# Eight units of a selective scan added by VectorE instead of twelve, and other places for the work between the scans

## The chip, the cores and the metric

One core of a Trainium2 chip runs the whole program. The metric is the device time of one execution in microseconds, from the start to the end of the program; the time of the kernel before is the median of three runs.

## The reference

Two layers in a row over x of shape (2, 4096, 512), in float32.

```python
def mixer(x, ...):                       # d_model 512, d_inner 1024, d_state 16, conv width 4, dt_rank 64
    xz = einsum('bld,ed->ble', x, in_proj_w);  xs, z = split(xz)
    xs = silu(causal_conv4(xs, conv_w) + conv_b)
    dt, B, C = split(einsum('bld,ed->ble', xs, x_proj_w), [64, 16, 16])
    dt = softplus(einsum('blr,dr->bld', dt, dt_proj_w) + dt_proj_b)
    A = -exp(A_log)                      # (1024, 16)
    h[t] = exp(dt[t] * A) * h[t-1] + dt[t] * B[t] * xs[t]      # state (1024, 16) for each batch
    y[t] = sum_n h[t][:, n] * C[t][n] + xs[t] * D
    return einsum('bld,ed->ble', y * silu(z), out_proj_w)
def ffn(x, ...):                         # weights quantised to -1, 0, 1
    return einsum('bsf,df->bsd', relu(einsum('bsd,fd->bsf', x, Wq1) + b1), Wq2) + b2
x = layernorm(x + mixer(x));  x = layernorm(x + ffn(x))
```

## The kernel before, in words

The program has two phases, one after the other. The change touches the first (`mixer_phase`) alone; `ffn_phase` is the same in both kernels.

**Tiling.** The 8192 tokens are cut into 16 chunks of 512, taken from the two batches in turn. In a chunk the 1024 channels are 8 blocks of 128 (the partitions), in 4 pairs q. A *unit* u (0 to 63) is one pair q = u // 16 and one state n = u % 16: two scans over 512 tokens, one for each block j of the pair. The body of a chunk is written once for every engine (`chunk`), as a loop over the 64 units; the first and the last chunk stand alone and the others are in a hardware loop of two chunks a turn. p, c and f are the chunk before, this one and the next: beside the scans of c run the output projection, residual and norm of p, and the input projection, convolution, x projection, dt projection and softplus of f.

**One unit through the engines.**
- ScalarE, `decay` (L488): exp(dt * A) into PSUM, one for each scan. There are two such banks; the decay of scan k waits until scan k - 2 is done.
- GpSimd, the product (L445): `dbu` = `dtx` * B for both blocks, in two buffers; it waits until both scans of unit u - 2 are done. In front of it GpSimd saves the last column of unit u - 2 (`carry`, L419).
- VectorE, `scan` (L696): twice a unit, into one of three slots of `h`. In front of the first it waits for the product, for the transposes and the carry of the unit that had the slot (three units back in most cases), and for the decay.
- TensorE, `transpose_h` (L871): four transposes for each half k of the unit, into PSUM `ht`, each half followed by one slot of other matmuls (`SLOTS`: two passes of 512 columns). The transposes wait for both scans of their unit, and for the reader of `ht` of the unit before.
- The reader multiplies by C. For most units it is ScalarE (`scale_by_c`, L502: four instructions of 128x256 into `ch`), and TensorE then adds the eight blocks to PSUM `y` (`sum_over_n`, L876). For the units in `BY_DVE` it is VectorE (`add_by_c`, L713 and L717: four instructions of 128x256 that add into `ya` in SBUF), and TensorE takes `ya` in only once for each pair q, at its last unit.

**The other work** stands at places written out by hand, one table for each operation (`TAKE_X`, `CONV_AT`, `ROUND_AT`, ...), each keyed by the unit u after whose instructions it is issued. On ScalarE: the first tap of the convolution (L510), SiLU of x (L516, four instructions and a table load), takes of PSUM banks (`take_xd` L521, `take_ct` L525, `take_dt` L532, `take_z` L552), the exponential of the softplus (L539 and L541), its logarithm (L546), SiLU of z (L557), and the norm's (L562, L566, L570). On VectorE: three taps a block and the copy that gives the bank back (L659, L667), `softplus_round` (L676, the rounding, and L678, the lift, behind one another), `softplus_sum` (L684), `skip` (L724), residual, statistics and shift (L731, L736, L742, L748). On GpSimd: the excess of the softplus (L384), `make_dtx` (L392), the gate with z (L379), the correction of the convolution (L400 to L413). SP issues all DMAs: B rows of a unit, weights of a block, tokens.

**Order on VectorE before.** In unit u: the statistics where they are due; scan 0; taps 2 and 3 of a block; the add of unit u - 1, if VectorE has it (for units 10, 38, 54 and 60 it stands in front of scan 0 of the next, `ADD_FIRST`); scan 1; then tap 1, skips, rounding with lift, sum, residual and shift. On ScalarE in unit u: decay of u + 1 and scaling of u - 1 for k = 0, the same for k = 1, and then all the rest that is due at u.

## Time and profile before

| | us |
|---|---|
| median of three runs | 5273.15 (5272.78 to 5276.83) |
| profiled execution, its own time | 5271.46 |
| its span, first to last instruction | 5269.7 |
| first scan of the first chunk | 83.8 |
| first scan of the sixth chunk, and of the seventh | 1347.3, 1601.5 |
| last scan ends | 4143.4 |

The rows are from one profiled execution. In a view of groups, a row gives line, engine, operation, output and inputs, the shape, the count, the busy time, the mean ns of one, and the idle time of the engine just before them with what ended it. In the timeline, a row gives start and length in us, and in brackets how long the engine had been idle and what released it. Busy times of windows are unions; the matmul records overlap one another at their ends, so what one costs TensorE is read from the distance of starts.

### The profile page before, as it was taken

To read this page: it belongs to the slowest core of one execution; us is meant where nothing else is said; L and a number is where in the kernel's file an instruction comes from. 1 tells how busy PE (TensorE), PEld (TensorE's weight loads), DVE (VectorE), ACT (ScalarE), POOL (GpSimd) and SP (SyncE) were. 2 spreads that over 40 slices of the span, in tenths; PEclk is the share of its full clock that TensorE was granted. 3 is DMA by queue.
4 is the path that set the end of the run, shared out by engine and by line. 5 is a ranking of instruction groups with operands and counts; after the bars stand their busy time and mean duration, and the time that the engine had idled before them with its cause. 6 is when DMAs were issued, how large, how long until landed. Compare 5 with 4: busy or idle time off the path is not lost. (4 is left out here: it accounts for less than half of the span.)

```text
span 5269.7 us, 85222 instructions
## 1 busy us (share of the span) xinstructions
PE 4539.6 (86%) x23362; PEld 3148.9 (60%) x23362; DVE 4053.4 (77%) x4775; ACT 3573.7 (68%) x6726; POOL 3171.4 (60%) x2474
## 2 busy tenths in 40 slices
PE   5989897988888888879797979797987579999998
PEld 3656555555555555656564656565656357777777
DVE  5888888888888888888898989898988554444444
ACT  5888787878787878787887787878787412222222
...
GB/s 96 97 91 91 100 92 99 90 99 92 104 86 107 95 97 93 96 98 91 97 96 104 84 101 87 103 89 101 88 91 89 130 2 32 41 39 32 32 32 32
DMA packets 233272, 436.64 MB, mean 83 GB/s; under 512 B 23872, under 2 KB 24000, under 8 KB 232320
## 3 DMA queue, kind: packets, MB, share of 16 engines
...
## 5 line engine op out<-in xcount | busy, mean ns | idle before, releaser
L696 DVE TENSOR_TENSOR_SCAN h<-decay,carry,dbu 128x512 f32<-128x512 f32 x2048 | 2528.8, 1269 | 313.6 <-ACT decay L488 144.4
L445 POOL TENSOR_TENSOR dbu<-dtx,bb 128x1024 f32<-128x1024 f32 x1024 | 2462.3, 2405 | 5.5 <-issue 2.2
L488 ACT ACTIVATE decay<-dt,aneg 128x512 f32<-128x512 f32 x2048 | 1431.3, 701 | 692.6 <-DVE h L696 688.0
L871 PE MATMUL ht<-ident,h 128*128 128x128 f32 x8192 | 1338.9, 291 | 609.7 <-DVE h L696 462.2
L871 PEld LDWEIGHTS ht<-ident,h 128*128 128x128 f32 x8192 | 1012.0, 149 | 1329.4 <-issue 812.6
L502 ACT ACTIVATE ch<-ht,ct 128x256 f32<-128x256 f32 x3328 | 1404.0, 482 | 93.3 <-PE ht L871 91.5
L821 PE MATMUL gemm<-xt,win 128*128 128x512 f32 x2048 | 1067.6, 606 | 10.8 <-DMA win<-w_in 7.1
L876 PEld LDWEIGHTS y<-ident,ch 128*128 128x128 f32 x6656 | 790.3, 143 | 407.3 <-issue 364.1
L876 PE MATMUL y<-ident,ch 128*128 128x128 f32 x6656 | 893.1, 278 | 4.2 <-ACT ch L502 1.9
L419 POOL TENSOR_TENSOR carry<-h,ones_pair 128x2 f32<-128x2 f32 x1022 | 272.0, 266 | 856.7 <-DVE h L696 846.9
L1119 ACT ACTIVATE hr<-hidden_ps,b1c 128x512 f32<-128x512 f32 x256 | 176.4, 689 | 715.8 <-PE hidden_ps L1252 715.8
L855 PE MATMUL gemm<-wout,x 128*128 128x512 f32 x1024 | 529.3, 604 | 0.0
L1201 DVE CAST hhi<-hr 128x512 fp32r<-128x512 f32 x256 | 109.3, 427 | 496.1 <-ACT hr L1119 496.0
L1263 PE MATMUL out_ps<-w2q,hhi 128*128 128x512 f32 x1024 | 409.1, 400 | 2.8 <-DVE hlo L1203 2.6
L1252 PE MATMUL hidden_ps<-xhi,w1q 128*128 128x512 f32 x1024 | 407.4, 398 | 1.4 <-DVE xlo L1164 1.4
L1252 PE MATMUL hidden_ps<-xlo,w1q 128*128 128x512 f32 x1024 | 407.3, 398 | 0.0
L1263 PE MATMUL out_ps<-w2q,hlo 128*128 128x512 f32 x1024 | 404.0, 395 | 0.0
L821 PEld LDWEIGHTS gemm<-xt,win 128*128 128x128 f32 x2048 | 319.3, 196 | 28.0 <-issue 20.9
L717 DVE SCALAR_TENSOR_TENSOR ya<-ht,ct,ya 128x256 f32<-128x256 f32 x512 | 221.4, 477 | 120.9 <-PE ht L871 119.8
L659 DVE SCALAR_TENSOR_TENSOR x<-gemm,cw,x 128x511 f32<-128x511 f32 (+2 forms) x384 | 281.3, 733 | 20.8 <-ACT x L510 16.0
L1263 PEld LDWEIGHTS out_ps<-w2q,hhi 128*128 128x128 f32 x1024 | 193.4, 189 | 54.0 <-issue 8.6
L1252 PEld LDWEIGHTS hidden_ps<-xhi,w1q 128*128 128x128 f32 x1024 | 193.0, 189 | 50.3 <-DVE xlo L1164 1.8
...
## 6 DMA issues: line engine op xcount, KB each, us to landing
bb<-b_rows SPq DMA_DIRECT2D x1024, 256.0 KB, 3.3
win<-w_in SPq DMA_DIRECT2D x256, 256.0 KB, 3.7
...
```

The source lines that it names most:

```text
L419: nc.gpsimd.tensor_tensor(carry[:, c.par, n, pair(q)], h[:, H_SLOT[u], :, TC - 1], ones[:, :], ALU.mult)\
L445: nc.gpsimd.tensor_tensor(dbu[:, u % 2, :, :], dtx[:, pair(q), :], bb[:, u % BB_RING:u % BB_RING + 1, :].to_broadcast([P, 2, TC]), ALU.mul ...
L488: nc.scalar.activation(DA[j][:, :], dt[:, c.par, i, :], ACT.Exp, scale=aneg[:, i, n:n + 1])\
L502: ins = nc.scalar.activation(ch[:, b % 2, tb, :], HT[k][:, tb % 2, :], ACT.Copy, scale=ct[:, c.par, tb, n:n + 1])
L659: nc.vector.scalar_tensor_tensor(x[:, f.par, i, back:], G[BANK["x", i]][:, 0:TC - back], cw[:, i, KC - 1 - back:KC - back], x[:, f.par, i, ...
L696: nc.vector.tensor_tensor_scan(h[:, H_SLOT[u], j, :], DA[j][:, :], dbu[:, u % 2, j, :], carry[:, c.par, n, i:i + 1], ALU.mult, ALU.add).th ...
L821: ins = nc.tensor.matmul(G[BANK[kind, i]][:, :], win[:, slot, k, :], xt[:, chunk.par, k, :], start=(k == 0), stop=(k == KM - 1))
L855: ins = nc.tensor.matmul(G[BANK["o", tb]][:, :], x[:, p.par, i, tb * P:(tb + 1) * P], wout[:, i, :], start=(i == 0), stop=(i == NB - 1))
L871: ins = nc.tensor.transpose(HT[k][:, tb % 2, j * P:(j + 1) * P], h[:, H_SLOT[u], j, tb * P:(tb + 1) * P], ident[:, :])
L876: return nc.tensor.matmul(Y[j][:, tb * P:(tb + 1) * P], src, ident[:, :], start=begins and tb == 0, stop=False, is_transpose=True, skip_gr ...
L1252: ins = nc.tensor.matmul(HP[j % 2][:, :], w1q[:, k, j * P:(j + 1) * P], part[:, k, :], start=(k == 0 and part is xhi), stop=(k == KM - 1 a ...
L1263: ins = nc.tensor.matmul(OP[tb][:, :], part[:, j % 2, tb * P:(tb + 1) * P], w2q[:, j, :], start=(j == 0 and part is hhi), stop=(j == NJ - ...
```

## The change

`BY_DVE` goes from twelve units to eight, and the tables give finer places. ScalarE's are keyed by 2u + k (after half k of unit u), VectorE's by 3u + s (s = 0 in front of scan 0, 1 between the scans, 2 behind scan 1), GpSimd's by u as before. Every add has a place of its own in `ADD_AT` (`ADD_FIRST` is gone), every tap, statistic and skip too, and the lift is split from the rounding, with its own semaphore. The tables for TensorE and SP are the same.

```diff
-BY_DVE = (9, 10, 20, 37, 38, 39, 53, 54, 55, 59, 60, 61)
-ADD_FIRST = (11, 39, 55, 61)
+BY_DVE = (9, 21, 39, 51, 52, 53, 55, 59)
...
-TAKE_X = {20 + 2 * i: i for i in range(NB)}
-CONV_AT = {21 + 2 * i: i for i in range(NB)}
-SILU_X_AT = 37
-TAKE_Z = {3: 0, 36: 1, 38: 2, 44: 3, 52: 4, 54: 5, 56: 6, 58: 7}
-TAKE_XD_AT, TAKE_CT_AT = 43, 46
-TAKE_DT = {47 + i: (2 * i, 2 * i + 1) for i in range(NB // 2)}
-EXP_AT = {48: 0, 50: 1, 3: 2, 5: 3}
-ROUND_AT = {50: 0, 52: 1, 5: 2, 7: 3}
-LN_AT = {53: (0, 1), 9: (2, 3)}
-EXCESS_AT = {56: 0, 57: 1, 12: 2, 13: 3}
-DT_SUM_AT = {56: 0, 57: 1, 12: 2, 13: 3}
-DTX_AT = {60: 0, 61: 1, 4: 2, 6: 3, 18: 4, 20: 5, 22: 6, 24: 7}
-SILU_Z_AT = 59
-GATE_AT = {61: (0, 1), 62: (2, 3), 63: (4, 5), 3: (6, 7)}
-SKIP_AT = {NS * (q + 1) + 2: q for q in range(NP - 1)}
-RESIDUAL_AT = {7 + 4 * tb: tb for tb in range(TB)}
-STATS_AT, NORM_LN_AT, SHIFT_AT = 39, 53, 54
-NORM_AT = {56: (0,), 57: (1, 2), 58: (3,)}
-CORR_AT, FIX_AT = 2, 38
+TAKE_X = {41: 0, 45: 1, 47: 2, 53: 3, 58: 4, 60: 5, 65: 6, 68: 7}
+SILU_X_AT = 80
+TAKE_Z = {8: 0, 72: 1, 76: 2, 91: 3, 109: 4, 113: 5, 115: 6, 116: 7}
+TAKE_XD_AT, TAKE_CT_AT = 85, 92
+TAKE_DT = {94: (0, 1), 95: (2,), 96: (3,), 97: (4,), 100: (5, 6), 101: (7,)}
+EXP_AT = {2: 2, 9: 3, 97: 0, 102: 1}
+LN_AT = {21: (2, 3), 105: (0, 1)}
+SILU_Z_AT = 118
+NORM_LN_AT = 105
+NORM_AT = {111: (0,), 113: (1,), 117: (2,), 121: (3,)}
+ADD_AT = {32: 9, 68: 21, 124: 39, 159: 51, 161: 52, 168: 53, 170: 55, 183: 59}
+CONV_AT = {65: ((0, 1),), 66: ((0, 2),), 67: ((0, 3),), 69: ((1, 1),), 71: ((1, 2),), 73: ((1, 3),), 76: ((2, 1),),
+           79: ((2, 2),), 82: ((2, 3),), 85: ((3, 1), (3, 2)), 87: ((3, 3),), 93: ((4, 1),), 94: ((4, 2), (4, 3)), 96:
+           ((5, 1),), 97: ((5, 2),), 98: ((5, 3),), 101: ((6, 1),), 103: ((6, 2),), 105: ((6, 3),), 106: ((7, 1), (7,
+           2)), 110: ((7, 3),)}
+ROUND_AT = {23: (2,), 29: (3,), 151: (0,), 160: (1,)}
+LIFT_AT = {14: (2,), 30: (3,), 156: (0,), 158: (1,)}
+DT_SUM_AT = {36: 2, 48: 3, 177: 0, 180: 1}
+SKIP_AT = {7: ((3, 0), (3, 1)), 54: ((0, 0),), 56: ((0, 1),), 105: ((1, 0), (1, 1)), 152: ((2, 0),), 154: ((2, 1),)}
+RESIDUAL_AT = {26: 0, 37: 1, 48: 2, 64: 3}
+STATS_AT = {85: (0,), 96: (1,), 114: (2,), 115: (3,)}
+NORM_SUMS_AT, SHIFT_AT = 151, 167
+EXCESS_AT = {12: 2, 15: 3, 56: 0, 57: 1}
+DTX_AT = {1: (2,), 11: (3,), 16: (4,), 18: (5,), 20: (6,), 25: (7,), 60: (0,), 61: (1,)}
+GATE_AT = {3: (6,), 6: (7,), 60: (0, 1), 61: (2,), 62: (3, 4), 63: (5,)}
+CORR_AT, FIX_AT = 10, 39
...
-                wait(act, rounded_ready, f, 2 * NP, 2 * q + 2)
+                wait(act, rounded_ready, f, NP, q + 1)
+                wait(act, lifted, f, NP, q + 1)
...
                 if j == 0:
-                    wait(dve, dbu_ready, c, UNITS, u + 1)
                     back, user = h_user_before(u)
                     wait(dve, ht_full, c.near(back), HALVES, 2 * user + 2)
                     wait(dve, carried, c.near(back), UNITS, user + 1)
+                    wait(dve, decay_ready, c, SCANS, 2 * u + 1)
+                    wait(dve, dbu_ready, c, UNITS, u + 1)
+                else:
+                    wait(dve, decay_ready, c, SCANS, 2 * u + 2)
...
                 for u in range(UNITS):
+                    between(3 * u)
                     scan(c, u, 0)
+                    between(3 * u + 1)
                     scan(c, u, 1)
+                    between(3 * u + 2)
```

`between(at)` issues what is due at `at` in the order add, taps, skips, roundings, lifts, sum, residual, statistics, their aggregation, shift.

## Rows read from the trace of the kernel before

**Rows 1.** The page: busy us, share of the span and instructions of each engine.

```profile
PE 4539.6 (86%) x23362; PEld 3148.9 (60%) x23362; DVE 4053.4 (77%) x4775; ACT 3573.7 (68%) x6726; POOL 3171.4 (60%) x2474
```

**Rows 2.** Windows: busy us of PE, PEld, DVE, ACT, POOL, then PEclk, DMA share, GB/s.

```profile
1347.30:1393.60 46.30, 41.49 (x234) 28.24 (x233) 39.36 (x41) 39.06 (x73) 41.05 (x35) 0.97 0.32 104
1393.60:1431.60 38.00, 36.86 (x203) 24.67 (x202) 33.22 (x32) 27.05 (x58) 32.98 (x25) 0.96 0.24 77
1431.60:1481.30 49.70, 47.85 (x271) 32.23 (x270) 49.42 (x59) 42.26 (x90) 36.42 (x30) 1.00 0.31 104
1481.30:1510.90 29.60, 22.41 (x107) 13.71 (x106) 23.99 (x37) 20.00 (x33) 15.27 (x14) 0.88 0.23 77
1510.90:1578.10 67.20, 59.42 (x319) 37.67 (x318) 56.24 (x55) 59.16 (x116) 50.59 (x37) 0.97 0.26 80
1578.10:1601.50 23.40, 10.49 (x63) 8.19 (x61) 17.34 (x22) 18.65 (x30) 22.30 (x19) 0.72 0.54 169
```

**Rows 3.** Groups by line of VectorE and ScalarE, in one chunk, 1347.3 to 1601.5.

```profile
L696 DVE TENSOR_TENSOR_SCAN h<-decay,carry,dbu 128x512 f32<-128x512 f32 x128 | 158.0, 1269 | 20.0 <-ACT decay L488 8.7 <-POOL carry L419 6.5 <-POOL dbu L445 3.7
...
L717 DVE SCALAR_TENSOR_TENSOR ya<-ht,ct,ya 128x256 f32<-128x256 f32 x32 | 13.9, 478 | 8.0 <-PE ht L871 8.0
...
L713 DVE TENSOR_SCALAR ya<-ht,ct 128x256 f32<-128x256 f32 x16 | 7.0, 479 | 5.6 <-PE ht L871 5.6
...
L676 DVE TENSOR_SCALAR rounded<-soft 128x1024 f32<-128x1024 f32 x4 | 4.8, 1210 | 0.0
...
L502 ACT ACTIVATE ch<-ht,ct 128x256 f32<-128x256 f32 x207 | 87.2, 481 | 4.0 <-PE ht L871 3.9
```

**Rows 4.** Timeline of TensorE, unit 14 and the start of 15.

```profile
1405.38 0.60 PE L871 MATMUL ht<-ident,h 128*128 128x128 f32 x4
...
1407.99 1.04 PE L876 MATMUL y<-ident,ch 128*128 128x128 f32 x8
...
1408.87 0.60 PE L871 MATMUL ht<-ident,h 128*128 128x128 f32 x4
```

**Rows 5.** Groups by line of VectorE in units 36 to 42, 1481.3 to 1510.9.

```profile
L717 DVE SCALAR_TENSOR_TENSOR ya<-ht,ct,ya 128x256 f32<-128x256 f32 x8 | 3.5, 480 | 3.2 <-PE ht L871 3.2
...
L736 DVE BATCH_NORM_STATS2 stats<-xres 128x6 f32<-128x512 f32 x4 | 2.5, 679 | 0.0
...
L713 DVE TENSOR_SCALAR ya<-ht,ct 128x256 f32<-128x256 f32 x4 | 1.8, 480 | 0.9 <-PE ht L871 0.9
```

**Rows 6.** Timeline of GpSimd at the end of the chunk, two products.

```profile
1589.05 2.35 POOL L445 TENSOR_TENSOR dbu<-dtx,bb 128x1024 f32<-128x1024 f32 x1
...
1593.94 2.36 POOL L445 TENSOR_TENSOR dbu<-dtx,bb 128x1024 f32<-128x1024 f32 x1
```

**Rows 7.** Timeline at SiLU of x, and TensorE after an idle time.

```profile
1489.98 1.28 ACT L516 ACT_TABLE_LOAD   x1
...
1491.27 3.90 ACT L516 ACTIVATE x<-x 128x1024 f32<-128x1024 f32 x4
...
1496.49 1.30 ACT L488 ACTIVATE decay<-dt,aneg 128x512 f32<-128x512 f32 x2
...
1502.07 1.11 PE L871 MATMUL ht<-ident,h 128*128 128x128 f32 x4 [5.75 <-DVE h L696]
```

**Rows 8.** Timeline at units 48 and 49, what ends just before a scan.

```profile
1524.86 2.36 POOL L445 TENSOR_TENSOR dbu<-dtx,bb 128x1024 f32<-128x1024 f32 x1
...
1527.54 2.46 DVE L696 TENSOR_TENSOR_SCAN h<-decay,carry,dbu 128x512 f32<-128x512 f32 x2 [0.34 <-POOL carry L419]
...
1530.39 0.79 ACT L488 ACTIVATE decay<-dt,aneg 128x512 f32<-128x512 f32 x1
...
1531.21 2.62 DVE L696 TENSOR_TENSOR_SCAN h<-decay,carry,dbu 128x512 f32<-128x512 f32 x2 [1.21 <-ACT decay L488]
```

**Rows 9.** One line each: rounding and dt sum, ns min/median/max.

```profile
L676 DVE TENSOR_SCALAR rounded<-soft x64: 665/895/2250, 67.6 to 3944.0; 128x1024 f32<-128x1024 f32 x64
L684 DVE SCALAR_TENSOR_TENSOR dt<-soft,dt x64: 1190/1199/3343, 74.4 to 3970.4; 128x1024 f32<-128x1024 f32 x64
```

More of the change, by code:

```diff
@@ L228, in mixer_phase @@
         rounded_ready = sem("rounded_ready")
+        lifted = sem("lifted")
         ln_ready = sem("ln_ready")
@@ L634, in _ @@
+                        if at == NORM_LN_AT and not is_first:
+                            norm_ln(p)
+                            norm_exp(p)
+                        if not is_first:
+                            for tb in NORM_AT.get(at, ()):
+                                norm_apply(p, tb)
+                        if at == SILU_Z_AT:
+                            silu_z(c)
             walk(act, chunk)
@@ L757, in _ @@
                 softplus_round(first, q)
+                softplus_lift(first, q)
             for q in (0, 1):
```

151 lines of the change are left out of this document (74 added, 77 removed).

## The prediction

> **What bounds the kernel now.** I read the page first. It shows four engines at 60 to 86 per cent of the whole span [rows 1], an average over two programs: the page's chain of waits runs through the second phase, which the change leaves alone. The first phase has sixteen chunks, and its clock is the start of VectorE's scans. So I took one chunk without a disturbance, from 1347.3 to 1601.5 us, 254.2 us long, and asked the view of windows for six stretches of it [rows 2]: units 0 to 12, 12 to 22, 22 to 36, 36 to 42, 42 to 59 and 59 to 64. The reader is to see that the limit moves. In the second and third TensorE is busy 36.9 of 38.0 and 47.9 of 49.7 us, and VectorE 49.4 of 49.7. In the fourth nobody is (VectorE 24.0 of 29.6). In the fifth ScalarE leads (59.2 of 67.2), VectorE just behind (56.2). In the last it is GpSimd (22.3 of 23.4). Over the chunk VectorE works 219.6 us and is idle for some 34.6. The groups by line [rows 3] say before what: 20.0 us before scans (8.7 for a decay, 6.5 and 3.7 by GpSimd), and 8.0 + 5.6 = 13.6 us before the adds of the twelve units, always for TensorE's transposes.
>
> **TensorE's floor.** A full unit is four transposes, a slot, four transposes, a slot and eight summing transposes; in the timeline the next unit starts at 1408.87 after 1405.38, which is 3.49 us, of which the eight summing ones are 0.88 (1407.99 to 1408.87) [rows 4]. A unit added by VectorE has no such sum and costs 2.61. Units 0 to 35 fill every slot: 36 x 3.49 = 125.6, plus three sums of `ya` and two dropped units' difference: after, 125.6 + 3 x 0.88 - 2 x 0.88 = 126.5 us (before 125.6, with three dropped). They take 134.0 us now (the first three windows).
>
> **Part 1, eight units instead of twelve.** VectorE loses 16 instructions. 48 of them are busy 13.9 + 7.0 = 20.9 us [rows 3], 0.435 each: -7.0 us of its work a chunk. ScalarE gets 16 scalings at 87.2 / 207 = 0.42 [rows 3]: +6.7 us. TensorE gets 4 sums, +3.5 us. None of the three is a change of time by itself; each counts in the stretch where that engine is last.
>
> **Part 2, adds later.** An add now stands between the two scans one unit on, or in front of them. Its transposes need both scans of its unit and then stand on either side of a slot, so VectorE comes too early for each half: in units 36 to 42 it idles 3.2 + 0.9 us before the pieces of three adds [rows 5]. The new places are one scan to two units later, when the transposes are there. I take 10 of the 13.6 us as gone and 3.6 as staying (unit 55's, unit 39's).
>
> **Part 3, by stretch.** *Units 0 to 36.* The wait for units 9, 10 and 20 goes, and the two exponentials, two roundings and gates that stand close together in units 3 to 7 are spread. But TensorE leaves only 134.0 - 126.5 = 7.5 us to win. Against that stand new waits: the sum of `dt` is now in front of unit 12's scan, and needs an excess that GpSimd makes after that unit's product; it is late by about one half product, 1.4 us (a product is 2.35) [rows 6]. Taps of the convolution are spread over more units, so the banks of blocks 2 and 6 are given back later, 1 to 2 us for TensorE. I take -4.0; bounds 0 and -7.5.
> *Units 36 to 42.* Out go the adds of 37 and 38 (8 x 0.435 = 3.5), the statistics of two blocks and the aggregation (1.5, moved into earlier units where TensorE covers them) and the 4.1 us of waits before adds; four statistics are busy 2.5 us [rows 5]. In comes a bare SiLU of x. It takes ScalarE from 1489.98, a table load of 1.28 and 3.90 of work, and then another load, to the next decay at 1496.49 [rows 7]: 6.5, with a decay on each side 7.8 us from the scan that releases it to the one it releases. Now the adds of 37 and 38 and the statistics cover it. After, only scan, scan (1.2 from one to the next: three in a row are over in 3.6) and the add of 39 (4 x 0.435) lie beside it: 1.2 + 1.2 + 1.7 = 4.1. Uncovered 3.7. Sum -3.5 - 1.5 - 4.1 + 3.7 = -5.4; bounds -1.3 (none of the waits goes) and -9.1 (SiLU hidden).
> *Units 42 to 59.* One more add here, so VectorE +1.7, ScalarE 1.7 less. The take of xd stands one unit earlier, at the end of unit 42, and TensorE ends that product only then; ScalarE holds the next decays behind it: +2.2. The exponentials now stand between two decays of one unit instead of after both, so VectorE has one scan less as cover. Against that the waits before three adds go. I take +1.5; bounds -6 and +7.
> *Units 59 to 64.* GpSimd has five products, two `dtx` and six gates before and after. From one product to the next with two gates between is 1593.94 - 1589.05 = 4.89 us [rows 6] and it is busy 22.3 of the 23.4 us [rows 2]; moving gates within five units frees nothing. SiLU of z stands half a unit earlier with less cover, but it hides behind GpSimd: +0.5; bounds -1 and +2.
>
> **Part 4, the product waited for last.** The scan's waits are separate; the last one is cheap. A decay ends at 1530.39 + 0.79 = 1531.18 and the scan starts at 1531.21, 0.03 us later; a product ends at 1524.86 + 2.36 = 1527.22 and its scan starts at 1527.54, 0.32 us later [rows 8]. That second row names the carry as releaser, but the carry is three units old and passed; it is the product. So 0.29 is to be had where the 3.7 + 6.5 us of waits for GpSimd stand, at some twelve places, 3.5 us; where GpSimd or TensorE is last, it isn't passed on. I take -0.5 (bounds 0 and -3.5).
>
> **Part 5, GpSimd's own instructions** change in place, not in number: no DMA is moved, and SP's queue keeps its order; only its waits for banks follow TensorE.
>
> **Sum.** -4.0 - 5.4 + 1.5 + 0.5 - 0.5 = -7.9 us a chunk. Each new place has its own small release, which I price at +0.5: -7.4. The first chunk has no norm before it and the last no next chunk, so fifteen of sixteen: 15 x -7.4 = -111. The profiled execution took 5271.5 us (its span 5269.7 and 1.8 around it); it is 1.7 below the median 5273.15. 5273 - 111 = 5162, and I say **5160 us**. The bounds add up to -27 and +8 a chunk; five errors seldom fall together, so the forecast's own range goes a quarter of the way to each, -12 and -3.5: 5273 - 15 x 12 = 5093 to 5273 - 15 x 3.5 = 5220.
>
> **A rule weighed: who holds the port.** A rounding takes from 665 to 2250 ns, a `dt` sum from 1190 to 3343, for one shape [rows 9]. In this chunk the four roundings average 1210 [rows 3], so 4 x 0.545 = 2.2 us are waits inside them, and if one sum of the four is of the long sort, 2.15 more: 4.3. "SBUF — State Buffer" of the Trainium skill, section "SBUF: two separate sides", says that a VectorE operation in a two-port mode or with two SBUF inputs and a GpSimd operation exclude one another, and that whichever starts first keeps the pair to its end. By that rule the trace agrees (the excess is of a product's length), and the change isn't neutral: the lift stood right behind its rounding, and now takes its turn alone. I left this out of the sum, since the places behind a second scan come before the next product starts, and the two roundings between scans come in the midst of one.
>
> **Rivals.**
> *A: smaller gain, 5240.* TensorE takes back nearly all of units 0 to 36 (-1), SiLU and the take of xd cost what they can: -1 - 3 + 2.3 - 0.5 = -2.2; 15 x -2.2 = -33. For: TensorE has +3.5 us more and is at 96 per cent in two windows. Against: 36 to 42 doesn't hang on it. Chance 0.19.
> *B: larger gain, 5035.* The first stretch reaches TensorE's floor, SiLU is half hidden, and the fifth gains a little: -7.5 - 7 - 1 - 0.5 = -16; 15 x -16 = -240. For: after an idle of 5.75 us, TensorE's four transposes take 1.11 instead of 0.60 [rows 7, 4], and the granted clock of the windows with such gaps is 0.88 and 0.72 [rows 2], between its levels of 1.2 and 2.4 GHz; shorter gaps give that back. Against: four engines within 10 per cent of each other. Chance 0.13.
> *C: slower, ScalarE late.* The mechanism is that exponentials, SiLU and xd stand between two decays of one unit; VectorE has one scan (1.2) to cover 2.1 to 6.5 us. If cover is what the old places had, units 36 to 59 lose 2.2 (xd) + 3 x 1.2 + 3.7, less the 4 that the adds give back: +5.5, and the first stretch gives nothing: 5273 + 15 x 5.5 = 5355. It decides where the waits before scans for a decay pass 20 us a chunk (8.7 now). For: ScalarE is at 59.2 of 67.2 already. Against: its load there falls by 1.7. Chance 0.08.
> *D: slower, the port.* If each of the twelve roundings, lifts and sums waits out half a product (1.2), that is 14.4 for 4.3: +10, which eats the -7.4: 5273 + 15 x 2.7 = 5314. The page of the Trainium skill named above, "SBUF — State Buffer", is where this comes from. It decides when the mean excess of the twelve is over (4.3 + 7.4) / 12 = 0.98 us. Against: eight of twelve stand where a scan has just ended. Chance 0.05.
> *E: nothing,* the parts cancel within 0.2 per cent, 10.5 us, which is about what a measurement of this kernel can tell from no change: 5273, 0.04.
>
> **How the numbers follow.** Forecast 0.51, A 0.19, B 0.13, C 0.08, D 0.05, E 0.04. Faster by over 0.2 per cent: 0.51 + 0.19 + 0.13 = 0.83; same 0.04; slower 0.13. The range leaves 0.10 above (C and most of D) and 0.10 below (the far part of B): 5070 to 5265; the forecast's own is 5093 to 5220.
>
> **What would show it.** Right: the idle before `ya` falls under 4 us a chunk; stretch 36 to 42 takes 22 to 25 us; 59 to 64 stays at 23 to 24; releases by the product come at 0.03 to 0.1; TensorE is idle under 4 us in units 12 to 36. Wrong: stretch 42 to 59 over 72 us (C); the mean rounding over 1.7 us or lift over 1.6 (D); or units 0 to 36 not under 132 us, which would mean that TensorE's floor was hit from another side.

## The result, and the profile after

The kernel after takes 5245.74 us, median of five runs (5234.61 to 5249.39), beside 5273.15 (5270.68 to 5291.18) for the kernel before on the same chip: a ratio of 0.9937, 95% interval 0.9918 to 0.9957. That is 27 us less. The forecast was 5160, 113 less; the time lies inside the range given (5070 to 5265), and next to rival A's 5240. The direction was right, and the size was four times too large: that the time lies inside the range says little, since the range also held rival A.

The profiled execution of after took 5243.3 us. The page's line of busy times answers to [rows 1]:

```profile
PE 4566.3 (87%) x23874; PEld 3192.9 (61%) x23874; DVE 3851.1 (73%) x4519; ACT 3673.4 (70%) x6982; POOL 3179.2 (61%) x2474
```

VectorE has 202 us less to do, ScalarE 100 more, TensorE 27 more. Now one chunk in the six stretches of [rows 2], 1355.7 to 1608.5 (252.8 us). The columns are busy us of PE, PEld, DVE, ACT and POOL, then the clock, the DMA share and GB/s:

```profile
1355.70:1400.70 45.00, 40.88 (x225) 27.95 (x226) 37.38 (x37) 40.13 (x77) 38.45 (x34) 0.96 0.31 98
1400.70:1435.80 35.10, 34.49 (x196) 23.31 (x195) 29.70 (x29) 28.57 (x63) 32.86 (x25) 1.00 0.24 73
1435.80:1489.10 53.30, 50.24 (x287) 33.98 (x286) 51.76 (x66) 41.14 (x85) 35.58 (x28) 1.00 0.38 110
1489.10:1512.90 23.80, 20.84 (x117) 13.44 (x115) 18.22 (x21) 22.32 (x40) 15.34 (x13) 1.00 0.30 93
1512.90:1583.40 70.50, 59.74 (x307) 37.08 (x308) 54.83 (x64) 58.70 (x114) 50.30 (x37) 0.95 0.24 73
1583.40:1608.50 25.10, 13.36 (x83) 11.69 (x81) 14.85 (x17) 21.83 (x38) 23.23 (x19) 0.80 0.44 145
```

Three stretches are shorter than in [rows 2] and three longer: 46.3, 38.0, 49.7, 29.6, 67.2, 23.4 became 45.0, 35.1, 53.3, 23.8, 70.5, 25.1. One chunk of each can mislead, since chunks of one execution differ (250.4 to 256.8 us in after, 253.7 to 262.8 in before). So the next table has the means of fourteen chunks (the second to the fifteenth), from start to start of the scans that bound the stretches; it also holds the experiments, in the order in which they come below. The last column is the whole run.

```
us per chunk    0-6   6-12  12-22  22-36  36-42  42-52  52-59  59-64   chunk   ratio [95%]
before        24.61  23.81  38.06  49.78  29.42  35.90  31.17  23.71  256.46   1
after         21.25  23.21  35.41  53.25  23.84  39.70  31.75  26.21  254.62   0.9937 [0.9918, 0.9957]
a_wait        21.91  23.03  35.67  53.22  23.83  39.38  31.46  26.37  254.86   0.9960 [0.9946, 0.9973]
b_wait        24.00  23.68  38.07  49.36  29.20  36.29  31.22  23.65  255.46   0.9968 [0.9955, 0.9981]
a_xd          21.60  22.94  35.20  53.27  23.84  38.16  32.68  26.17  253.86   0.9903 [0.9887, 0.9918]
a_zg          22.15  23.39  35.52  53.27  23.83  39.62  31.64  24.67  254.08   0.9905 [0.9889, 0.9921]
a_conv        21.42  23.27  34.44  52.11  24.54  39.47  31.49  26.38  253.11   0.9883 [0.9865, 0.9902]
b_by8         24.02  22.48  39.94  50.03  25.97  38.83  30.56  23.28  255.12   0.9940 [0.9923, 0.9956]
h2            22.21  23.60  34.75  52.11  24.54  38.08  32.09  25.52  252.89   0.9867 [0.9849, 0.9884]
h3            22.59  22.94  34.40  52.11  24.54  41.52  30.14  25.54  253.78   0.9921 [0.9905, 0.9937]
b_by8w        23.98  22.47  38.81  49.68  25.95  39.17  30.18  23.06  253.31   0.9914 [0.9901, 0.9927]
a_stats       21.32  22.94  35.19  52.31  24.16  39.45  31.93  26.31  253.61   0.9931 [0.9919, 0.9944]
h6            20.68  23.41  34.75  50.94  25.92  39.19  30.18  23.07  248.14   0.9751 [0.9738, 0.9763]
h7            21.35  23.21  34.51  50.95  26.50  38.20  32.66  23.38  250.76   0.9821 [0.9808, 0.9835]
```

Before to after: units 0 to 22 -6.6, 22 to 36 +3.5, 36 to 42 -5.6, 42 to 59 +4.4, 59 to 64 +2.5: -1.8 a chunk. Fourteen such chunks give -26; the first is 5.2 longer, the last 9.2 shorter and the first scan 2.1 later, so the last scan ends at 4115.8 where it was 4143.4: -27.6. Each row of the table is one profiled execution, and how far its cells can be trusted shows in units 0 to 22: the ten kernels with the new places there take 78.8 to 81.1 us for them, the four with the old ones 85.3 to 86.5. So the 6.6 us are real, and a difference under some 1 us in that stretch is not.

What VectorE waits for has changed hands. Two rows of the page for the scan, first before, then after (busy us, mean ns, idle us just before, and the releaser with the most of it):

```profile
L696 DVE TENSOR_TENSOR_SCAN h<-decay,carry,dbu 128x512 f32<-128x512 f32 x2048 | 2528.8, 1269 | 313.6 <-ACT decay L488 144.4
```

```profile
L714 DVE TENSOR_TENSOR_SCAN h<-decay,carry,dbu 128x512 f32<-128x512 f32 x2048 | 2538.3, 1270 | 593.9 <-ACT decay L497 416.6
```

And in the chunk of the windows, the groups that answer to [rows 3]:

```profile
L714 DVE TENSOR_TENSOR_SCAN h<-decay,carry,dbu 128x512 f32<-128x512 f32 x129 | 160.0, 1270 | 40.7 <-ACT decay L497 26.3 <-POOL dbu L454 8.9 <-issue 4.8
...
L511 ACT ACTIVATE ch<-ht,ct 128x256 f32<-128x256 f32 x224 | 93.9, 477 | 7.4 <-PE ht L898 7.3
...
L731 DVE TENSOR_SCALAR ya<-ht,ct 128x256 f32<-128x256 f32 x16 | 6.8, 473 | 2.3 <-PE ht L898 2.2
L735 DVE SCALAR_TENSOR_TENSOR ya<-ht,ct,ya 128x256 f32<-128x256 f32 x16 | 6.7, 473 | 2.2 <-PE ht L898 2.2
```

(The 4.8 us of "issue" are one gap, just in front of the chunk's first scan; over the fourteen chunks they come to 0.3 a chunk.) The reader is to see three things. The adds wait 4.5 us where they waited 13.6: that part came as planned. The adds' work fell from 20.9 to 13.5 us, as planned too. But the scans wait 26.3 us for a decay of ScalarE where it was 8.7. In the fourteen-chunk means VectorE works 207.3 us a chunk where it worked 220.5, and its idle time rose from 35.9 to 47.3 (for a decay 9.4 to 27.0, before adds 13.6 to 5.3): most of what was taken from VectorE became waiting for ScalarE.

**Where ScalarE comes late.** The take of xd, in the timeline of after; it stands behind the second decay of unit 43 and in front of the first of unit 44:

```profile
1516.31 0.85 ACT L511 ACTIVATE ch<-ht,ct 128x256 f32<-128x256 f32 x2
...
1518.49 1.02 PE L858 MATMUL gemm<-x,wxp 128*96 128x512 f32 x2
...
1519.55 0.60 ACT L530 ACTIVATE rounded<-gemm 96x512 f32<-96x512 f32 x1 [2.39 <-PE gemm L858]
1520.05 0.67 ACT L497 ACTIVATE decay<-dt,aneg 128x512 f32<-128x512 f32 x1
...
1520.85 1.28 DVE L714 TENSOR_TENSOR_SCAN h<-decay,carry,dbu 128x512 f32<-128x512 f32 x1 [2.75 <-ACT decay L497]
```

ScalarE itself stands idle for 2.39 us, because TensorE ends the x projection only at 1519.51; the decay behind the take comes late by that, and the first scan of unit 44 waits 2.75 (3.5 in the mean of fourteen chunks). The second place is SiLU of z, between the decays of unit 60:

```profile
1585.85 0.70 ACT L497 ACTIVATE decay<-dt,aneg 128x512 f32<-128x512 f32 x1
...
1586.85 1.28 DVE L714 TENSOR_TENSOR_SCAN h<-decay,carry,dbu 128x512 f32<-128x512 f32 x1
1587.32 1.28 ACT L567 ACT_TABLE_LOAD   x1
...
1588.61 3.90 ACT L567 ACTIVATE z<-z 128x1024 f32<-128x1024 f32 x4
1589.83 2.50 POOL L388 TENSOR_TENSOR x<-x,z 128x512 f32<-128x512 f32 x2 [1.77 <-ACT z L567]
...
1592.43 2.35 POOL L454 TENSOR_TENSOR dbu<-dtx,bb 128x1024 f32<-128x1024 f32 x1
1592.53 1.28 ACT L497 ACT_TABLE_LOAD   x1
1593.82 0.69 ACT L497 ACTIVATE decay<-dt,aneg 128x512 f32<-128x512 f32 x1
...
1594.55 1.28 DVE L714 TENSOR_TENSOR_SCAN h<-decay,carry,dbu 128x512 f32<-128x512 f32 x1 [6.42 <-ACT decay L497]
...
1595.32 1.12 PE L898 MATMUL ht<-ident,h 128*128 128x128 f32 x4 [7.31 <-ACT ch L511]
```

Decay, a scaling, load, SiLU, load, decay are one row on ScalarE, and VectorE has only the scan of 1.28 us beside them: it stands 6.42 us, TensorE 7.31. GpSimd's product for the next unit is late as well, since it is queued behind gates that wait for z (1.77 idle, and the product starts only at 1592.43).

**Table loads.** Each of the 164 loads of this trace takes 1.28 us, and here each starts 0.02 us behind the instruction before it and the next one 0.01 us behind the load, so SiLU with both loads is 1.28 + 3.90 + 1.28 = 6.5 us. "ScalarE: Activation LUTs" of the Trainium skill, section "What ACT_TABLE_LOAD costs", gives the same 1283 ns for the load but adds a drain to some 2.66 us for each switch; by that the piece would be 9.2. This trace doesn't show the drain, and the measurement decides.

### The profile page after: what moved, and what is told of

It is laid out like the page before. It is cut to its first block and busy times, and to the rows that moved or that the text cites. A ratio compares the mean times of both kernels' runs of the same rounds, so it can differ in the third digit from the quotient of the medians.

```text
span 5241.6 us, 86246 instructions
## 1 busy us (share of the span) xinstructions
PE 4566.3 (87%) x23874; PEld 3192.9 (61%) x23874; DVE 3851.1 (73%) x4519; ACT 3673.4 (70%) x6982; POOL 3179.2 (61%) x2474
## 5 line engine op out<-in xcount | busy, mean ns | idle before, releaser
L898 PE MATMUL ht<-ident,h 128*128 128x128 f32 x8192 | 1301.6, 284 | 469.0 <-ACT ch L511 330.9
L898 PEld LDWEIGHTS ht<-ident,h 128*128 128x128 f32 x8192 | 992.4, 146 | 1131.1 <-ACT ch L511 581.5
L511 ACT ACTIVATE ch<-ht,ct 128x256 f32<-128x256 f32 x3584 | 1505.9, 479 | 122.3 <-PE ht L898 120.9
L903 PEld LDWEIGHTS y<-ident,ch 128*128 128x128 f32 x7168 | 860.9, 145 | 443.3 <-issue 403.1
L848 PE MATMUL gemm<-xt,win 128*128 128x512 f32 x2048 | 1083.9, 614 | 20.9 <-DVE hist L679 13.7
L903 PE MATMUL y<-ident,ch 128*128 128x128 f32 x7168 | 976.1, 280 | 12.4 <-DVE x L741 12.0
L428 POOL TENSOR_TENSOR carry<-h,ones_pair 128x2 f32<-128x2 f32 x1022 | 258.0, 252 | 814.0 <-DVE h L714 802.0
L1279 PEld LDWEIGHTS hidden_ps<-xhi,w1q 128*128 128x128 f32 x1024 | 193.1, 189 | 50.3 <-DVE xlo L1191 1.8
L1279 PEld LDWEIGHTS hidden_ps<-xlo,w1q 128*128 128x128 f32 x1024 | 193.1, 189 | 47.0
```

Of the source, the lines that this page charges most:

```text
L428: nc.gpsimd.tensor_tensor(carry[:, c.par, n, pair(q)], h[:, H_SLOT[u], :, TC - 1], ones[:, :], ALU.mult)\
L511: ins = nc.scalar.activation(ch[:, b % 2, tb, :], HT[k][:, tb % 2, :], ACT.Copy, scale=ct[:, c.par, tb, n:n + 1])
L848: ins = nc.tensor.matmul(G[BANK[kind, i]][:, :], win[:, slot, k, :], xt[:, chunk.par, k, :], start=(k == 0), stop=(k == KM - 1))
L898: ins = nc.tensor.transpose(HT[k][:, tb % 2, j * P:(j + 1) * P], h[:, H_SLOT[u], j, tb * P:(tb + 1) * P], ident[:, :])
L903: return nc.tensor.matmul(Y[j][:, tb * P:(tb + 1) * P], src, ident[:, :], start=begins and tb == 0, stop=False, is_transpose=True, skip_gr ...
L1279: ins = nc.tensor.matmul(HP[j % 2][:, :], w1q[:, k, j * P:(j + 1) * P], part[:, k, :], start=(k == 0 and part is xhi), stop=(k == KM - 1 a ...
```

## The experiments

Theory T1: the adds and statistics of VectorE had covered ScalarE's long pieces, and what the change takes off VectorE's path there comes back as waiting for a decay. T2: ScalarE's load (the sum of its work) is a floor in units 42 to 64, whatever the places. The rival to both: the order of the scan's waits, or TensorE, took the gain back. T1 and T2 mean these two down to b_by8w, whose expectation gives them another wording.

**a_wait and b_wait: the order of the scan's waits.** a_wait is after with the old order, b_wait before with the new one. In b_wait:

```diff
                 if j == 0:
-                    wait(dve, dbu_ready, c, UNITS, u + 1)
                     wait(dve, ht_full, c.near(back), HALVES, 2 * user + 2)
                     wait(dve, carried, c.near(back), UNITS, user + 1)
+                    wait(dve, decay_ready, c, SCANS, 2 * u + 1)
+                    wait(dve, dbu_ready, c, UNITS, u + 1)
+                else:
+                    wait(dve, decay_ready, c, SCANS, 2 * u + 2)
-                wait(dve, decay_ready, c, SCANS, 2 * u + j + 1)
```

> The changed kernel with the old order of waits in front of the first scan (product first, decay last). Theory 'the order pays': each of some 9 releases by the product in a chunk costs 0.29 us more, the period of a chunk grows by 1 to 2.5 us, and the time from 5246 to 5260-5285, over the kernel before. Rival 'another engine is last there': under 0.5 us a chunk, 5240-5253; the releases are later and TensorE or GpSimd hides it.

> The kernel before with the new order of waits alone (product last). Theory 'the order pays': the 3.8 + 4.6 us of waits for GpSimd a chunk fall by up to 3.5, the time by 15 to 50, to 5225-5258. Rival 'another engine is last': 5265-5275, the waits only change their name.

Measured: a_wait 0.9960 [0.9946, 0.9973], b_wait 0.9968 [0.9955, 0.9981]. The order alone makes the kernel before 0.3% faster, 16 us; taken out of after it costs about 0.2%, with intervals that overlap. Neither expectation was met cleanly: b_wait's 5263 lies between its two bands, and a_wait's 5258 is 2 us short of the theory's, while its chunk grows by only 0.2 us, which is the rival's mark. What the order does to a single release is clear. In after a product that comes last releases its scan 0.04 us after its end (1602.23 + 2.37 = 1604.60), where [rows 8] had 0.32:

```profile
1602.23 2.37 POOL L454 TENSOR_TENSOR dbu<-dtx,bb 128x1024 f32<-128x1024 f32 x1
...
1604.64 2.46 DVE L714 TENSOR_TENSOR_SCAN h<-decay,carry,dbu 128x512 f32<-128x512 f32 x2 [2.46 <-POOL dbu L454]
```

Over the whole traces, the scans that had to wait for their product start 0.32 us behind its end in before and a_wait (median of 188 and 129) and 0.035 us in after and b_wait (141 and 174). So the order didn't take the gain back. In b_wait it is worth 1.0 us a chunk, twice the 0.5 that the prediction took; in after its worth is not settled.

**a_xd: the take of xd one unit later.**

```diff
-TAKE_XD_AT, TAKE_CT_AT = 85, 92
+TAKE_XD_AT, TAKE_CT_AT = 87, 92
```

> The changed kernel with one edit: the take of xd one unit later, after unit 43 (TAKE_XD_AT 85 to 87), as in the kernel before. Theory 'work between decays': the 3.3 us wait in unit 43 falls under 1, units 42 to 52 go from 39.7 to 36.5-37.5 us, the time from 5246 to 5195-5220. Rival 'ScalarE's load': it has 16 scalings more whatever their place, so units 42 to 52 stay at 39-40 and the time within 10 us.

Measured: 0.9903 [0.9887, 0.9918], 5232 us, 13 under after and outside both bands. The wait in front of unit 44, 3.5 us, is gone, and units 42 to 52 are 1.5 shorter (38.2 where 36.5 to 37.5 was expected); 0.9 of it comes back in 52 to 59. The wait was a matter of place, but of 3.5 us only 0.6 stay as a gain in 42 to 59. That the rest comes back is not shown to be ScalarE's load, as T2 has it: in units 42 to 59 of this kernel ScalarE is busy 58.9 of 70.8 us, and 6.0 of its idle time are waits for TensorE's transposes in front of a scaling.

**a_zg: SiLU of z and the gates at their old places.**

```diff
-SILU_Z_AT = 118
+SILU_Z_AT = 119
-GATE_AT = {3: (6,), 6: (7,), 60: (0, 1), 61: (2,), 62: (3, 4), 63: (5,)}
+GATE_AT = {3: (6,), 6: (7,), 61: (0, 1), 62: (2, 3), 63: (4, 5)}
```

> The changed kernel with SiLU of z at the end of unit 59 (118 to 119) and the gates where they were (two after each of units 61, 62, 63), as in the kernel before. Theory 'work between decays': the 6.4 us wait in unit 60 falls to 2-3.5, GpSimd's product of unit 61 no longer stands behind two gates, units 59 to 64 go from 26.2 to 23-24 us, the time from 5246 to 5200-5220. Rival 'GpSimd's sum is the floor': the stretch has the same five products, two dtx and six gates, and stays at 25-26; time within 10 us.

Measured: 0.9905 [0.9889, 0.9921], 5231 us, 11 above the expected band. Units 59 to 64 give 1.5 of the 2.5 us that they had lost (24.7 for the 23 to 24 expected), but in this trace units 0 to 22 are 1.2 longer, so the chunk is 0.5 shorter. The first scan of unit 61, which now stands behind SiLU of z, still waits 5.1 us. The add of unit 60, which had lain there, is not in the list of eight; h6 and h7 below show what it makes of that wait.

**a_conv: the convolution as before.** The first taps stand four half units apart again, and the other taps of a block close together.

```diff
-TAKE_X = {41: 0, 45: 1, 47: 2, 53: 3, 58: 4, 60: 5, 65: 6, 68: 7}
-CONV_AT = {65: ((0, 1),), 66: ((0, 2),), 67: ((0, 3),), 69: ((1, 1),), 71: ((1, 2),), ...
+TAKE_X = {41 + 4 * i: i for i in range(NB)}
+CONV_AT = {65: ((0, 1),), 67: ((0, 2), (0, 3)), 71: ((1, 1),), 73: ((1, 2), (1, 3)), ...
```

> The changed kernel with the convolution where it was: first taps on ScalarE after every second unit from 20, VectorE's first tap behind the second scan, the other two and the copy between the next unit's scans. Theory 'banks': the spread taps give a bank back up to two units later, and TensorE, the last engine here, waits for the copy; undone, units 22 to 36 go from 53.3 to 49.7-50.3 us, the time from 5246 to 5190-5210. Rival 'TensorE's floor': its extra sums make 14 x 3.49 + 0.9 = 49.7 us anyway, and what is lost was lost before; the stretch stays above 52, time within 10 us.

Measured: 0.9883 [0.9865, 0.9902], 5220 us, 26 under after, the largest step by the places of one operation. It misses the 5190 to 5210 of the theory, and units 22 to 36 take 52.1 us where the theory had 49.7 to 50.3 and the rival over 52. 1.1 us came from units 22 to 36 and 1.0 from 12 to 22 (which is within what that stretch varies by); 36 to 42 paid 0.7. So the spread taps cost something, and are a third of what units 22 to 36 had lost, not all of it.

**b_by8: the kernel before with eight adds, nothing moved.**

```diff
-BY_DVE = (9, 10, 20, 37, 38, 39, 53, 54, 55, 59, 60, 61)
-ADD_FIRST = (11, 39, 55, 61)
+BY_DVE = (9, 20, 37, 38, 53, 54, 59, 60)
+ADD_FIRST = (39, 55, 61)
```

> The kernel before with four units fewer on VectorE (10, 39, 55 and 61 go to ScalarE) and nothing moved. Theory 'the adds were cover': VectorE works 7.0 us less a chunk, but at 39, 55 and 61 ScalarE is in a long block (SiLU, logarithm), so waits for a decay rise from 9.0 by about what the adds lose: the chunk moves by less than 2 us, 5250-5290, and only units 6 to 12 shrink. Rival 'work is work': VectorE is the most loaded engine, and 4 to 7 us a chunk go, 5170-5215.

Measured: 0.9940 [0.9923, 0.9956], 5248 us, the gain of the whole change, by two lines; 2 us under the theory's band and far above that of "work is work". Its scans wait 13.4 us a chunk for a decay and not 27.0. The expectation that only units 6 to 12 shrink failed in a way that matters: units 36 to 42 fall by 3.5 us, and 42 to 52 grow by 2.9, though in 42 to 52 nothing was moved and no add was dropped. TensorE is about half a unit further behind when unit 42 starts (40.4 units transposed where it was 41.0), and in 42 to 52 it is busy 38.2 of 38.8 us (before 35.3 of 35.9). ScalarE is busy 37.0 there and waits 1.5 for its transposes, where it waited for none. What the adds leave in 36 to 42 is for the most part taken back there, and TensorE is the engine that is full. So the other places of the change, taken together, bring nothing over this, although units 0 to 22 are 6.6 us shorter with them.

**h2 and h3: the mends together, with more adds.** h2 is after with the convolution, xd, SiLU of z and the gates as before, and units 60 and 61 added by VectorE as well (ten units). h3 is h2 with units 48 and 49 too; with unit 48 on VectorE no product starts PSUM `y` afresh for the last pair any more: h3 leaves out that start and the wait in front of it, and `y` of that pair is no longer the sum alone, so its time is of use only as a hint.

```diff
-BY_DVE = (9, 21, 39, 51, 52, 53, 55, 59)
-ADD_AT = {32: 9, 68: 21, 124: 39, 159: 51, 161: 52, 168: 53, 170: 55, 183: 59}
+BY_DVE = (9, 21, 39, 48, 49, 51, 52, 53, 55, 59, 60, 61)
+ADD_AT = {32: 9, 68: 21, 124: 39, 149: 48, 152: 49, 159: 51, 161: 52, 168: 53, 170: 55, 181: 59, 183: 60, 187: 61}
```

> The changed kernel with the three parts put right: convolution as before, take of xd after unit 43, SiLU of z and gates as before, and units 59, 60 and 61 added by VectorE (ten units; adds between the scans of 60, in front of 61, between the scans of 62). If the stretches add up: 79.9 (0 to 22, as changed) + 49.8 (22 to 36) + 23.8 + 70.8 (36 to 59, as with xd moved) + 23.7 = 248.0 us a chunk, 5246 - 15 x 6.6 = 5147, 5130-5170. Rival 'waits move': ScalarE is the floor from 42 on and takes back what 22 to 36 gives, 5190-5220.

> As the one with three parts put right, and VectorE adds units 48 and 49 too (behind the scans of 49 and 50), where it waits 2.9 and 3.6 us for ScalarE. Theory 'ScalarE is last in 42 to 52': its 8 scalings less, 3.4 us, shorten units 42 to 52 by 1.5 to 3.4 us: 5100-5140. Rival 'TensorE's lag': ScalarE waits there for dt blocks, nothing or a loss: 5140-5180.

Measured: h2 0.9867 [0.9849, 0.9884], 5209 us and not the 5147 expected; h3 0.9921 [0.9905, 0.9937]. Both miss. In h2 two stretches carry most of the miss: 22 to 36 takes 52.1 us, as in a_conv, for the 49.8 expected, and 59 to 64 takes 25.5 for 23.7. There the adds of 60 and 61 didn't help: a_zg, with the same places of SiLU of z and the gates and without these adds, takes 24.7. Two adds at 48 and 49 made 42 to 52 longer by 3.4 (and 52 to 59 shorter by 2.0): VectorE there waits 3.3 us until TensorE has finished `y` of the pair before. To put cover in wherever ScalarE is late does not work by itself.

**b_by8w: the two parts that had worked, together.** b_by8 with the wait order of b_wait.

> The kernel before with the eight adds (units 9, 20, 37, 38, 53, 54, 59, 60) at the old kind of place and the product waited for last; nothing else is moved. T1 (ScalarE's long pieces stand uncovered; the places of the change bring nothing net): the two parts that were measured alone add up, 0.9940 x 0.9968 = 0.991, that is about 5230 us, under the whole change's 5246. T2 (the new places carry the gain and only the order of the waits hides it): about 5248, as without the order.

Measured: 0.9914 [0.9901, 0.9927], 5229 us. 0.9940 x 0.9968 = 0.9908: the two add up, as its T1 has it, and this kernel is at 0.9914 where after is at 0.9937 (the intervals just overlap), though it moves nothing.

**a_stats: the statistics back in one place**, in front of unit 41's first scan.

```diff
-STATS_AT = {85: (0,), 96: (1,), 114: (2,), 115: (3,)}
-NORM_SUMS_AT, SHIFT_AT = 151, 167
+STATS_AT = {123: (0, 1, 2, 3)}
+NORM_SUMS_AT, SHIFT_AT = 123, 167
```

> The kernel after with the four blocks' statistics and their aggregation back in one place, behind unit 40's add (slot 123), where VectorE waits for the SiLU of x. Theory (VectorE is full in units 22 to 36, so work moved there is paid in full, while in 36 to 42 it had hidden SiLU): stretch 22 to 36 falls by 1.4 us (two blocks' statistics of 0.63 each and a little), 36 to 42 by 0.5 to 1.3 or at least doesn't grow, since the aggregation leaves 42 to 59: 2.0 to 2.6 us a chunk, 5205 to 5215 us. Rival (TensorE covers them there, as the prediction had it): 22 to 36 stays at 53.2 and 36 to 42 grows by up to 2.5: 5246 to 5285.

Measured: 0.9931 [0.9919, 0.9944]; the expected 5205 to 5215 was missed (5237). Units 22 to 36 fall by 0.9, two thirds of the 1.4 us of work that left them; 36 to 42 grow by 0.3 with four statistics and the sums in them where there were two, so most of what was put there lies beside SiLU of x. The theory's fall in 22 to 36 is there at two thirds, but it had 36 to 42 not growing, and the whole is within the interval of after. What is new in units 22 to 36 shows in VectorE's groups there, of after and then of before:

```profile
L714 DVE TENSOR_TENSOR_SCAN h<-decay,carry,dbu 128x512 f32<-128x512 f32 x29 | 36.1, 1267 | 1.4 <-ACT decay L497 1.4
...
L731 DVE TENSOR_SCALAR ya<-ht,ct 128x256 f32<-128x256 f32 x4 | 1.6, 468 | 0.0
...
L753 DVE BATCH_NORM_STATS2 stats<-xres 128x6 f32<-128x512 f32 x2 | 1.4, 684 | 0.0
```

```profile
L696 DVE TENSOR_TENSOR_SCAN h<-decay,carry,dbu 128x512 f32<-128x512 f32 x28 | 34.4, 1268 | 0.0
```

VectorE had no idle time before a scan here in the kernel before, and 1.4 us in the one after. The add of unit 21 (1.6) and two statistics (1.4) are new in the stretch, which grew by 3.5. By the runs most of that work is paid, though not all: 0.9 for the statistics (a_stats), 1.3 for the add (h6, below), and 1.1 for the taps (a_conv).

**h6: units 0 to 21 from after, the rest from before.** Units 0 to 21 as in after, everything from unit 22 on as in before (convolution too), the eight units 9, 21, 37, 38, 53, 54, 59, 60, and the new wait order. Against after:

```diff
-BY_DVE = (9, 21, 39, 51, 52, 53, 55, 59)
+BY_DVE = (9, 21, 37, 38, 53, 54, 59, 60)
-ADD_AT = {32: 9, 68: 21, 124: 39, 159: 51, 161: 52, 168: 53, 170: 55, 183: 59}
+ADD_AT = {32: 9, 68: 21, 115: 37, 117: 38, 163: 53, 165: 54, 181: 59, 183: 60}
-SILU_X_AT = 80
+SILU_X_AT = 75
-STATS_AT = {85: (0,), 96: (1,), 114: (2,), 115: (3,)}
-NORM_SUMS_AT, SHIFT_AT = 151, 167
+STATS_AT = {117: (0, 1, 2, 3)}
+NORM_SUMS_AT, SHIFT_AT = 117, 164
-SILU_Z_AT = 118
+SILU_Z_AT = 119
...
```

> The places of the kernel after for units 0 to 21, those of the kernel before from unit 22 on (convolution too), eight units added by VectorE (9, 21, 37, 38, 53, 54, 59, 60), the product waited for last. If the stretches are separate sums (theory: each place pays or costs where it stands), 0 to 22 takes the 80 us of after, 22 to 36 about 50.5, 36 to 64 what the eight units at old places gave (119): 249.5 us a chunk, about 5165 us. Rival (the gain of the first 22 units is time lent by the end of the chunk before, ScalarE and GpSimd being late there): 0 to 22 goes back toward 83 or 42 to 64 grows, in all 252 to 253 us, 5200 to 5220.

Measured: 0.9751 [0.9738, 0.9763], 5147 us, 99 under after and 126 under before, and 18 better than expected. Its stretches are those of after for 0 to 22 (78.8; after 79.9) and those of b_by8w behind (36 to 64: 118.4; 118.4). So the 6.6 us are not lent by the end of the chunk before. Units 22 to 36 take 1.3 more than in b_by8w, about the add of unit 21 that now lies in them. SiLU of z in this kernel:

```profile
1551.17 1.28 DVE L711 TENSOR_TENSOR_SCAN h<-decay,carry,dbu 128x512 f32<-128x512 f32 x1 [1.14 <-ACT decay L494]
...
1552.65 0.88 DVE L732 SCALAR_TENSOR_TENSOR ya<-ht,ct,ya 128x256 f32<-128x256 f32 x2 [0.20 <-PE ht L895]
1553.16 1.28 ACT L564 ACT_TABLE_LOAD   x1
...
1553.98 0.88 DVE L732 SCALAR_TENSOR_TENSOR ya<-ht,ct,ya 128x256 f32<-128x256 f32 x2 [0.46 <-PE ht L895]
1554.45 3.90 ACT L564 ACTIVATE z<-z 128x1024 f32<-128x1024 f32 x4
1554.78 1.27 DVE L711 TENSOR_TENSOR_SCAN h<-decay,carry,dbu 128x512 f32<-128x512 f32 x1
...
1556.97 1.66 DVE L732 SCALAR_TENSOR_TENSOR ya<-ht,ct,ya 128x256 f32<-128x256 f32 x4 [0.92 <-PE ht L895]
...
1560.48 4.81 DVE L711 TENSOR_TENSOR_SCAN h<-decay,carry,dbu 128x512 f32<-128x512 f32 x4 [1.85 <-ACT decay L494]
```

The same 6.5 us of ScalarE, but beside them lie the second scan of unit 60 and the four pieces of an add, with the rest of the add before just ahead: the scan waits 1.85 us and not 6.42.

**h7: h6 with the change's own eight units.**

```diff
-BY_DVE = (9, 21, 37, 38, 53, 54, 59, 60)
-ADD_AT = {32: 9, 68: 21, 115: 37, 117: 38, 163: 53, 165: 54, 181: 59, 183: 60}
+BY_DVE = (9, 21, 39, 51, 52, 53, 55, 59)
+ADD_AT = {32: 9, 68: 21, 124: 39, 159: 51, 161: 52, 168: 53, 170: 55, 183: 59}
```

> The kernel h6 with one thing put back: VectorE adds the change's eight units (9, 21, 39, 51, 52, 53, 55, 59) at the change's places in place of 9, 21, 37, 38, 53, 54, 59, 60; the pieces of ScalarE, GpSimd and the statistics stay where h6 has them. Theory (an add is worth most beside one of ScalarE's long pieces: 37 and 38 cover SiLU of x, 59 and 60 SiLU of z): SiLU of x and of z are each uncovered by one add (1.7 us), 36 to 42 doesn't fall although two adds (3.5 us of work) left it, 59 to 64 grows by 1 to 2, 42 to 59 by about 0 to 1: 1.5 to 3 us a chunk, 5170 to 5190 us. Rival (which units are added is indifferent, only the pieces' places cost): within 0.3 per cent of h6, 5147 us.

Measured: 0.9821 [0.9808, 0.9835], 5187 us, within the 5170 to 5190 expected and outside h6's interval. Which units VectorE adds, each at its place, is worth 0.7% (40 us), at equal work. The page's row for the scan, h6 and then h7:

```profile
L711 DVE TENSOR_TENSOR_SCAN h<-decay,carry,dbu 128x512 f32<-128x512 f32 x2048 | 2529.4, 1270 | 419.0 <-ACT decay L494 204.0
```

```profile
L711 DVE TENSOR_TENSOR_SCAN h<-decay,carry,dbu 128x512 f32<-128x512 f32 x2048 | 2533.2, 1271 | 512.5 <-ACT decay L494 326.6
```

Units 36 to 42 grew by 0.6 although one add (1.7 us of work) left them. The share of the two places was not as expected: 59 to 64 grew by 0.3 only, 42 to 59 by 1.5. The first scan of unit 61, behind SiLU of z, waits 5.2 us in h7 and 1.8 in h6, in the means: the adds of 59 and 60 are what covered it, but in that stretch wait and work nearly replace one another.

**The account.** From before, in ratios: eight adds at places like the old 0.9940, the wait order 0.9968, places of units 0 to 21 with the add at 21 for 20 (h6 to b_by8w) 0.9751 / 0.9914 = 0.984, the choice of units (h7 to h6) 1.007, the other places from unit 22 on (after to h7) 0.9937 / 0.9821 = 1.012. Undone one by one, convolution, xd, SiLU of z with gates, and statistics give 0.9946 x 0.9966 x 0.9968 x 0.9994 = 0.987, the inverse of 1.013; each of the four is taken from after's own ratio, whose interval of 0.2% so enters four times, and the agreement is a loose one. In the chunk means, one execution each, the four give 0.8 + 0.5 + 1.5 + 1.0 = 3.8 us and h7 lies 3.9 under after. The new places of the takes of `dt`, the exponentials, roundings and norm in units 47 to 60 were not tried alone.

## Why the prediction was wrong

In short: the prices of work and the waits before adds came nearly as told, but the sum over the stretches failed, most of all in units 42 to 59, where new waits of VectorE for ScalarE (8.0 us a chunk more) were put at next to nothing. "In the means" is over the fourteen chunks of the table, each kernel in one profiled execution.

*Part 1, the prices of work:* right. The adds' busy time fell by 7.4 us (forecast 7.0), ScalarE's scalings rose by 6.7 (93.9 for 87.2).

*Part 2, adds later:* right in the main: 13.6 us of waits for transposes became 4.5 to 5.3 (3.6 forecast, "under 4" set as the mark, missed by a little). In the means unit 39's is 2.5 and unit 55's 2.3, the two that were named. What failed is what these waits were worth in time, stretch by stretch.

*Part 3, units 36 to 42:* right in size, -5.6 for -5.4, in part by luck. VectorE's work fell by 5.6 us (5.0 forecast). Of 4.0 us of waits before adds 2.5 stayed, where all were taken as gone, and against that the waits for a decay are 2.9 and not the 3.7 taken for SiLU of x, and 1.2 of waits for GpSimd went that nobody had counted. And the aggregation of the statistics did not go "into earlier units": it stands in unit 50.

*Part 3, units 42 to 59: the term that failed most,* +1.5 forecast, +4.4 measured, 44 us of the 84 by which the chunks miss (15 x (7.4 - 1.8); 59 to 64 has 30, 0 to 36 has 14, 36 to 42 has -3; the order's and the releases' terms cancelled). Three steps failed.

1. "Against that the waits before three adds go": they are 2.0 us in before and 2.3 in after, in the means.
2. The exponentials between two decays were named and not priced, but the scans of this stretch wait 13.7 us for a decay where they waited 5.7. Of the 8.0 us more, the take of xd has 3.5 (it was priced at 2.2, and is 0.6 net in the stretch by a_xd). Another 1.6 stand behind the takes of `dt` between the decays of unit 48, which the prediction doesn't name, and 1.4 behind the exponential between those of unit 52; the other exponential of this stretch did not move (97 is the end of unit 48, where it was).
3. Each stretch was priced by itself, while b_by8 shows that what 36 to 42 gives is for the most part taken back in 42 to 52, with nothing moved there.

Behind the second stands something that the average over 42 to 59 in [rows 2] hid (ScalarE 59.2 of 67.2): in units 42 to 52 alone ScalarE is busy 35.6 of 35.9 us in before and TensorE 35.3, in the means. Two engines were full there, and by these busy times whatever makes one of them stand lengthens the stretch. In after ScalarE has no more to do (35.3 us of 39.7), but it stands 3.1 us for the x projection and 1.1 for a bank of `dt`, both TensorE's, and the stretch is 3.8 longer.

*Part 3, units 59 to 64: failed,* +0.5 forecast, +2.5 measured. "It hides behind GpSimd" didn't hold, for GpSimd's gates need z, and its products stand behind the gates: SiLU of z half a unit earlier, without the add of 60 beside it, stopped VectorE for 6.4 us, and the products of units 61, 62 and 63 start 5.4, 3.0 and 3.1 us later behind the first scan of unit 59 than in before, in the means; that of 63 then holds its scan for 2.5. a_zg, which puts both back, returns 1.5.

*Part 3, units 0 to 36:* -3.1 for -4.0, by two errors that cancel. Units 0 to 22 gave 6.6, more than all 36 were thought to: the chunk that was read takes 134.0 us for units 0 to 36 where the mean of fourteen is 136.3, so there was more to win above TensorE's floor, 9.8 us and not 7.5. Units 22 to 36 took back 3.5. The sentence that fails is "the statistics of two blocks ... moved into earlier units where TensorE covers them": VectorE was busy 49.42 of 49.7 us there [rows 2], and the statistics and the add of unit 21 that moved in cost 0.9 of 1.4 us (a_stats) and 1.3 of 1.6 (h6). The row stood in the prediction; it named two full engines and the sum used one. The taps, which the prediction did count, have 1.1 more (a_conv). The line drawn for it (132 us) was crossed, at 133.1: VectorE is busy 51.7 of 53.3 us in this stretch and TensorE 50.2, so it was hit from VectorE's side and, by the taps, perhaps from TensorE's too.

*Part 4, the wait order:* -0.5 taken of bounds 0 and -3.5; b_wait measured -1.0 a chunk; undone in a_wait it is 0.2 a chunk and 0.2% of the run.

*Rivals.* A's time was nearest, but its mechanism (TensorE takes the first stretch back) isn't what the trace shows: that stretch gave most. What TensorE takes back is in units 42 to 52 (b_by8). C's mechanism is what happened in half: its decision point, 20 us a chunk of waits for a decay, was passed (27.0), and 42 to 59 took 71.5 us where 72 was the mark; the kernel is not slower, since the first 22 units paid. D is refuted: its marks were a mean rounding over 1.7 us and a lift over 1.6. One line each of rounding, lift and sum in after, ns min/median/max, against [rows 9]:

```profile
L688 DVE TENSOR_SCALAR rounded<-soft x64: 664/668/762, 69.6 to 3930.3; 128x1024 f32<-128x1024 f32 x64
L694 DVE SCALAR_TENSOR_TENSOR dt<-dt,soft x64: 1191/1199/1256, 70.3 to 3930.9; 128x1024 f32<-128x1024 f32 x64
L700 DVE SCALAR_TENSOR_TENSOR dt<-soft,dt x64: 1196/1224/3505, 76.5 to 3952.1; 128x1024 f32<-128x1024 f32 x64
```

In fourteen chunks the mean rounding fell from 1264 to 673 ns, the lift from 1380 to 1207 and the sum from 1720 to 1383. The traces show why: in before 45 of the 64 roundings start while a GpSimd instruction of over 1 us is running, with a mean of 1465 ns, and the other 19 have 670; one that starts with 1.70 us of it left takes 2.25. In after only 15 do, with at most 0.08 us left. Only the sum still meets one now and then. The rule of "SBUF — State Buffer" of the Trainium skill, section "SBUF: two separate sides", that the one who started first keeps the pair, fits both traces; it was right to leave it out as a cost, and it turned out as a gain: rounding and lift take some 3 us less of VectorE's time a chunk.

*What stays open.* Why units 0 to 22 give 6.6 us is read from the trace only: before, VectorE waits 3.28 us for the transposes in front of the add of 20 and 2.3 in front of that of 9 and 10, and the roundings in units 5 and 7 are stretched; in units 0 to 6 its waits for GpSimd fall from 4.0 us to 1.1. No run took these apart. What in 42 to 52 takes back the time of 36 to 42 is read from the busy times and not from a run. And the second scan of unit 49 and the first of unit 50 wait 3.2 to 3.6 us a chunk for a decay in before, after, b_by8, b_by8w, h2, h6 and h7 alike; nothing was tried there but h3's two adds, which turned it into a wait for `y`.
